# Four images of a two-layer convolution and attention kernel: the image loops of all five engines written out

## The reference, cut to what matters

```python
def reference(x, ...):                       # x: (4, 384, 56, 56)
    # layer 0: depthwise 3x3 convs, sampled values, linear attention, 12 heads
    x = x + L0(gn(x))
    # layer 1: linear attention with 8 heads, and an MLP 384 -> 1536 -> 384
    x = x + L1(gn(x))

def L0(x):
    value, query = dwconv(x, w_v, 1), dwconv(x, w_q, 1)
    key, off = dwconv(x, w_k, 2), dwconv(x, w_off1, 2)        # stride 2: 28 x 28
    pos = tanh(gelu(layernorm(off)) @ w_off2 + ref_points)
    v_sampled = grid_sample_bilinear(value, pos)
    attn = einsum('bcm,bcn->bmn', query, key) * SCALE
    return w_out @ einsum('bmn,bcn->bcm', attn, v_sampled)

def L1(x):                                   # xs: tokens of x
    mid = silu(layernorm(xs) @ fc1_w + fc1_b) @ fc2_w + fc2_b
    q, k, v = heads(xs @ qkv_w);  q, k = q / |q|, k / |k|
    o = 0.5 * v + 1 / pi * q @ (k^T v);  o = o / |o| + mid
    return o @ proj_w + proj_b
```

## Time and profile before

| | |
|---|---|
| median of 3 executions | 2825.6 us (2822.07 to 2829.56) |
| the profiled execution | 2823.88 us |
| its span | 2822.1 us, 40251 instructions |
| TensorE | busy 2697.0 us (96%), mean granted clock 0.967 |
| VectorE, ScalarE, GpSimd | busy 1981.0 us (70%), 1176.4 us (42%), 658.5 us (23%) |
| chain that ended last | PE 71%, issue 10%, DMA 8%, DVE 6%, ACT 3%, POOL 2% |
| transfers | 347.62 MB, mean 123 GB/s |

### The profile page before, as it was taken

The page is one execution under the profiler, slowest core; times in us unless marked ns, Lnnn a source line. Parts: engine busy times, 40 slices in busy tenths (PEclk is TensorE's granted clock), DMA queues, the critical chain, the costliest instruction groups (busy, mean ns, idle before and its releaser), DMA issues.

```text
span 2822.1 us, 40251 instructions
## 1 busy us (share of the span) xinstructions
PE 2697.0 (96%) x14382; PEld 2447.3 (87%) x14382; DVE 1981.0 (70%) x2513; ACT 1176.4 (42%) x2039; POOL 658.5 (23%) x219
## 2 busy tenths in 40 slices
PE   6998799999999999999999999999999999999999
PEld 4556798899998899899998899899999899999998
DVE  5988785888887684988886674888887634434443
ACT  3432465444342465444432265444443254333332
POOL 0020142222222043222224033322224033211220
PEclk9998899999999999999999999999999999999999
DMA  5257632343338632333446743233436832112110
GB/s 222 58 156 258 216 96 81 102 110 113 103 101 255 219 123 82 101 101 101 107 120 200 261 129 100 70 103 110 122 101 178 281 110 79 43 43 52 47 43 30
DMA packets 208431, 347.62 MB, mean 123 GB/s; under 512 B 24288, under 2 KB 191840, under 8 KB 205408
## 3 DMA queue, kind: packets, MB, share of 16 engines
q1 hardware_dynamic: 182192, 311.60, 34.0%
q10 hardware_dynamic: 21552, 14.05, 3.7%
q0 software_dynamic: 4480, 19.27, 2.4%
HBM read 241.31 MB, written 103.56 MB: 122 GB/s over the span
## 4 chain that ended last, share of the span: by engine, by line
PE 71%; issue 10%; DMA 8%; DVE 6%; ACT 3%; POOL 2%; SPq 1%; ACTq 0%; DVEq 0%; POOLq 0%
PE bank L781 15%; PE bank L782 15%; PE bank L783 15%; PE bank L827 3%; PE bank L986 3%; PE bank L988 3%; PE bank L987 3%; PE bank L1177 3%; PE bank L1009 3%; PE bank L1163 2%; DVE AC L2391 2%; DMA r_scr<-rr 2%; POOL rq L701 1%; DMA X<-x_scr 1%; PE bank L1121 1%
## 5 line engine op out<-in xcount | busy, mean ns | idle before, releaser
L1751 ACT ACTIVATE S<-bank,b1p 128x448 f32<-128x448 f32 x336 | 212.4, 632 | 836.6 <-PE bank L783 795.1
L2391 DVE SCALAR_TENSOR_TENSOR AC<-XV,wfold,AC 128x1568 f32<-128x1568 f32 x288 | 530.0, 1846 | 2.8
L781 PE MATMUL bank<-SH,W2H 128*128 128x448 f32 x1008 | 391.3, 388 | 7.8 <-DVE SL L2360 7.7
L781 PE MATMUL bank<-XRH,W1H 128*128 128x448 f32 x1008 | 378.7, 376 | 0.7 <-ACT S L1751 0.7
L783 PE MATMUL bank<-SH,W2L 128*128 128x448 f32 x1008 | 375.9, 373 | 0.0
L782 PE MATMUL bank<-SL,W2H 128*128 128x448 f32 x1008 | 375.7, 373 | 0.0
L782 PE MATMUL bank<-XRL,W1H 128*128 128x448 f32 x1008 | 374.3, 371 | 0.0
L783 PE MATMUL bank<-XRH,W1L 128*128 128x448 f32 x1008 | 372.6, 370 | 0.0
L701 POOL TENSOR_TENSOR rq<-qn,nhalf 112x32 f32<-112x32 f32 x28 | 181.9, 6496 | 465.7 <-DVE qn L2330 465.7
L2360 DVE TENSOR_TENSOR SL<-S,SH 128x448 fp32r<-128x448 f32 x336 | 207.2, 618 | 92.4 <-ACT SH L1754 91.5
L705 POOL TENSOR_TENSOR ro<-on,nhalf 112x32 f32<-112x32 f32 x28 | 180.1, 6434 | 299.5 <-DVE on L2351 299.4
(11 more groups left out here) (228 smaller groups left out, 5171.9 us busy)
## 6 DMA issues: line engine op xcount, KB each, us to landing
XV<-in_xp SPq DMA_DIRECT2D x36, 870.0 KB, 7.3
XC<-in_xp SPq DMA_DIRECT2D x14, 1682.0 KB, 9.9
CQ<-q_scr SPq DMA_DIRECT2D x28, 672.0 KB, 7.1
CX<-in_x SPq DMA_DIRECT2D x28, 672.0 KB, 4.9
x_scr<-CX SPq DMA_DIRECT2D x28, 672.0 KB, 5.3
X<-x_scr SPq DMA_DIRECT2D x28, 672.0 KB, 4.2
V<-v_scr SPq DMA_DIRECT2D x28, 672.0 KB, 7.0
Y<-x_scr SPq DMA_DIRECT2D x28, 672.0 KB
```

What stands on the lines that cost most here:

```text
L781: mm(o, wh, xh, start=first, stop=False)
L1751: fn(S[:, j % 2, :], bank[j % 2][:, 0:T], ACT.Silu, bias=b1p[:, j:j + 1]).then_inc(s["s_s"], 1)
L2391: stt(o, XV[h][:, ky:ky + HR, kx:kx + W], wfold[:, kind, k, 3 * ky + kx:3 * ky + kx + 1], o, ALU.mult, ALU.add).then_inc(s["va"], 1)
```

## The change

On each engine the loop over images and the separate last image become one Python loop that writes all four images out. b is now a number in all four, so every wait and address that depends on it is a constant. On DVE the two one-pass loops go too. The inner loops of POOL stay loops. Operations, waits and their order are the same.

```diff
@@ sync @@
-            with sp.Fori(0, B - 1) as b:
-                image(b, True)
-            image(B - 1, False)
+            for b in range(B):
+                image(b, b < B - 1)
             sp.wait_ge(s["y_st"], HEAD + B * STRIPS * 16)
@@ gpsimd, tensor, scalar: the same edit @@
-            with pe.Fori(0, B - 1) as b:
-                image(b, True)
-            image(B - 1, False)
+            for b in range(B):
+                image(b, b < B - 1)
@@ vector @@
             def image(b, nxt):
-                for part in (keys_values, rest):
-                    if isinstance(b, int):
-                        part(b, nxt)
-                    else:
-                        with dve.Fori(b, b + 1) as c:
-                            part(c, nxt)
-
-            with dve.Fori(0, B - 1) as b:
-                image(b, True)
-            image(B - 1, False)
+                keys_values(b, nxt)
+                rest(b, nxt)
+
+            for b in range(B):
+                image(b, b < B - 1)
```

More of the change, by code:

```diff
@@ L739, in image @@
                     gn_rstd(b + 2)
-            with pool.Fori(0, B - 1) as b:
-                image(b, True)
-            image(B - 1, False)
+            for b in range(B):
+                image(b, b < B - 1)
         @block.tensor
@@ L1877, in image @@
                     tile(n0 + STRIPS - 1, STRIPS - 1)
-            with act.Fori(0, B - 1) as b:
-                image(b, True)
-            image(B - 1, False)
+            for b in range(B):
+                image(b, b < B - 1)
         @block.vector
```

## The result

The changed kernel takes 2807.5 us in the median of six runs (2802.2 to 2814.2), 0.9952 of the kernel before (95% interval 0.993 to 0.9975). The kernel before took 2821.7 and 2820.5 us beside it, and once 5983.5 us, an execution that is left out of the ratio; its three earlier ones are the 2825.6 us in the median of the forecast. Both intervals hold 0.9963 to 0.9975, that is 7 to 10 us less. The forecast was 2814.0 against 2825.6, a ratio of 0.9959.

What follows compares the result with a forecast made beforehand. TensorE, 71% of the chain, was taken to bound the kernel, standing still at loop back edges. 7.5 + 2.6 + 1.5 = 11.6 us off 2825.6 gave 2814.0 us, range 2809 to 2821.

Steps and rivals of the forecast that it cites:

- The boundary: Image ends, last matmul to key tile 1: each of two back edges costs 3.74 us, together 7.5 us saved.
- The clock: Key tile 0 after the second back edge: TensorE no longer falls to half clock, 2.6 us saved, bounds 0 to 2.6.
- The cover for ScalarE and VectorE: At the back edges: their work for the next image finishes before TensorE needs it, so their late starts cost nothing.
- Register work: Inside looped images: waits depending on b delay VectorE; five fc2 idles shrink by 0.29 us each, 1.5 us, bounds 0 to 3.
- Table loads: ScalarE at each looped image's head: three loads of 1283 ns may be spared; taken as 0, far end 1.3 us.
- The first, half a boundary: Image boundaries: only part of the gain comes back, half of 7.5 us giving 2821.9; value taken 2820 us; chance 0.16.
- The second, no effect: Image heads: the idles belong to something other than the jump and reappear; time stays 2825.6 us; chance 0.06.
- The third, new pauses in the text: Longer straight text: stalls on TensorE or SP, 12 x 2.25 = 27 us less the 11.6, giving 2841; chance 0.04.
- the sign that the prediction named: TensorE in the profile after: new issue idles there would show the prediction wrong.

Runs made afterwards that it cites:

- e1: Kernel before with only SyncE's loop over the images written out, the four other engines still looped; ratio 0.9962 to the kernel before, median 2815.2 us.
- e2: Kernel before with only TensorE's loop over the images written out; ratio 1.002 to the kernel before.
- e3: Kernel before with SyncE and TensorE written out, VectorE, ScalarE and GpSimd still looped; ratio 0.9973 to the kernel before.
- e7: Kernel before, all loops kept, SyncE loading the next image's key tile 1 ahead of the last output store and its jump; ratio 0.9998.
- e6: Kernel before without VectorE's two one-pass loops inside the image, all loops over the images kept; ratio 1.0.
- e4: Changed kernel, but VectorE keeps its loop over the images and its two one-pass loops; ratio 0.9963 to the kernel before.
- e5: Changed kernel plus a two-pass loop with one semaphore increment on SyncE between the last output store and next load; ratio 0.9977 to the kernel before.
- e9: Changed kernel plus one semaphore increment ahead of each of two VectorE taps in the first strip; ratio 0.9955 to the kernel before, median 2801.7 us.

## Why the prediction was right

**The boundary (7.5 us).** Right in size and cause. The exit from the loop was the right model: stretches of 11.38 and 11.40 us against its 11.45, 3.81 and 3.79 less than 15.19. e1, e2 and e3 show its structure: SP's late load and TensorE's late start stand one behind the other. TensorE's back edge taken away alone gives 0.1 to 0.2 us of stretch, SyncE's alone 0.2 and 2.4, and both together 2.7 to 2.8 even with the late landing of e3. What stands behind TensorE's own gap is the block of its text that comes in 1.8 to 1.9 us before it starts (e7). The key stages fell by 11.9 us in the first profile where this and the next term gave 10.1; 1.6 of that is the clock at another place.

**The clock (2.6 us).** Right for this profile: in image 2 tiles 1 and 2 now start 11.82 us apart, as at the exit, against 14.45 before. The figure is one profile's, though: in e6, whose loops over the images are those of before, the two distances are 13.40 and 13.39, so half clock cost 1.6 us behind each wait and not 2.6 behind one. e2 shows the other side: there the clock is at 0.50 behind a single wait of 5.0 us at both back edges.

**The cover for ScalarE and VectorE.** Right. Even with their back edges left in place (e3) both stand idle before their part of key tile 1, and what they wait for is the load. The term that the prediction had too simple is the load's time to land, which it took as 4.68 us at every boundary: it was 4.7 to 4.9 behind the back edges in the changed kernel and 5.2 to 5.9 in e1, e3 and e4, and there it sets the stretch wherever ScalarE waits for it.

**Register work (1.5 us, bounds 0 to 3).** The sum was nearly right by luck; the step was wrong. By the table, SyncE written out is worth 539.7 - 538.0 = 1.7 +- 0.9 us in each looped image, some 5 in all, and VectorE written out 538.0 - 534.3 = 3.7 +- 1.0 more, some 11 in all. Each alone is beyond my far end of 3. I had priced the one visible sign, 0.29 us, at the few places where TensorE waits for a split, and had SyncE's queue only as a bound. Rows 3, which gave the lower bound of 0, take the last pair of query norms of image 2, where the groups of the table do not differ either (64.1, 64.0, 63.9 us without the hole); the third and fourth strip do. Of the 5.4 us together, 4.0 +- 0.8 are lost again in the changed kernel; 2.5 of them stand in the second strip, where GpSimd waits, and the rest is not located. What is left is 1.4 +- 0.7 us per image, about 4 in all. No row of before could show the loss, since VectorE's loop, with which it does not appear, was in it.

**Table loads.** Four went, and no stretch shows them: 0, as taken.

**Rivals.** The first, half a boundary, did not come about: both stretches reached the exit's length. The second, no effect, is out by e1, e5 and the stretches. The third, new pauses in the text, needs a closer look. The row "L986 waits for issue" has no successor among the key products, but TensorE's list of waits has another row with issue, and ScalarE once stood far longer than the 2.25 us of the earlier trace rows (the second line is from the kernel before, the others from the changed one):

```profile
PE bank L1024 <- issue: 5.3, 3, 1.8
```

```profile
PE bank L1026 <- ACT KTS L1652: 5.4, 3, 1.8
```

```profile
2134.92 0.64 ACT L1748 ACTIVATE S<-bank,b1p 128x448 f32<-128x448 f32 x1 [9.11 <-issue]
```

The first is no new pause: the same three idles of 1.8 us stood before at the same place under another releaser. Beside it there are two small rows, 0.8 us in three idles at L1119 and 0.6 in one at L897. ScalarE's 9.11 us cost nothing that the trace shows, since TensorE was busy in all of the time from 2120 to 2140, and the pause is in no other profile. So by the sign that the prediction named, new issue idles of TensorE, 1.4 us appeared in the first profile; the 27 us of the rival did not. A loss at a new place there was, but of another kind, and smaller.

## What to carry to other kernels

The price of a loop's back edge is what stands behind each engine's jump: look first for the transfer that is issued after it, and treat jumps on several engines as waits in series: with TensorE's taken away alone, its time only fed the next wait. When a stretch comes out longer than planned, look first which engine waits for the transfer's landing, before it is put down to an engine's late start. If one pass of the loop already stands outside it, its boundary is the best estimate there is. After removing small delays on VectorE, look whether GpSimd's ops beside it got longer.

## What was not expected of the hardware

GpSimd's small power op (112 x 32) takes 5.43 us where no VectorE op is under way at its start, 6.97 beside VectorE's taps in most strips, and 9.26 beside the same ops in the second strip of the changed kernel; one semaphore increment ahead of each tap brings back 6.99. The Trainium skill, SBUF — State Buffer, SBUF: two separate sides, says that the two share a port pair as an exclusive lock, held by a VectorE op with two SBUF inputs for its whole length. GpSimd's side agrees: from the end of the first or of the third VectorE op its own takes 5.29 and 5.28 us, near the 5.43 of the undisturbed one. VectorE's side shows nothing of it: its second tap takes 1.84 us both where GpSimd's op seems to run beside it (before) and where it seems to wait (after). That GpSimd can be kept out over three ops is what e9 adds.

TensorE's gap at the same jump was 1.9 to 2.5 us with idle DMA engines and 3.5 us with a 576 KB load under way (e7). At all eight back edges of the four profiles it ended 1.81 to 1.90 us after a block of 16384 bytes had come in on TensorE's instruction queue, and this accounts for the two gaps of the kernel before, 2.46 and 1.90 us: the block of the first back edge started 0.5 us later than that of the second. Why it did is open.
